# Own rows left unscaled between the second and third pass of a four-layer graph kernel, and the squares shared by two engines

## The reference, cut to what matters

```
scores = h_src @ a_s + h_tgt @ a_t
mx = segment_max(scores, tgt);  ex = exp(scores - mx[tgt]);  se = segment_sum(ex, tgt)
agg = segment_sum(h_src * (ex / (se[tgt] + 1e-10))[:, None], tgt)
h_combined = h + agg
h_poincare = tanh(|h_combined|) * h_combined / |h_combined|     # per row
result = h_poincare, or h_poincare * 0.95 / (|h_poincare| + 1e-8) where the norm is over 0.95
```

## Time and profile before

| | |
|---|---|
| device time, median of 3 | 4950.73 us (4947.53 to 4952.23) |
| profiled execution: span from first to last instruction | 5717.0 us |
| what lies around that span in the profiled execution | not listed; its own time is read as the span |
| busy shares PE, PE weight load, DVE, ACT, POOL | 58%, 38%, 57%, 32%, 58% |
| mean granted TensorE clock | 0.754 |
| POOL, line 527 (own rows scaled) | 49 instructions, 44.1 us busy |

### The profile page before, as it was taken

How to read it: one execution, slowest core, us unless ns; L and a number is a source line. 1 busy time by engine, 2 the same in 40 slices (tenths; PEclk the granted TensorE clock), 3 DMA queues, 4 the chain that set the end, 5 groups by cost and what they waited for, 6 DMA issues and landing times. The chain is left out here.

```text
span 5717.0 us, 56211 instructions
## 1 busy us (share of the span) xinstructions
PE 3330.2 (58%) x11120; PEld 2187.6 (38%) x11120; DVE 3248.6 (57%) x10255; ACT 1811.1 (32%) x4253; POOL 3290.0 (58%) x3410
## 2 busy tenths in 40 slices
PE   0477777777543555556554555555555556666555
PEld 0355555555431333333333333333333334333333
DVE  8677777777983555555566344444447344334435
ACT  2254444444692323333336322222226100000000
POOL 5566666666004666666653666666662466666664
PEclk8789988898875777776777767777777776667767
DMA  2444444443114333333333444444443433333333
GB/s 90 118 110 111 110 110 107 110 111 106 49 46 123 92 91 93 94 89 93 92 101 119 111 111 113 114 112 112 114 111 114 143 98 99 93 98 101 99 91 107
DMA packets 290665, 586.90 MB, mean 103 GB/s; under 512 B 63201, under 2 KB 170717, under 8 KB 290334
## 3 DMA queue, kind: packets, MB, share of 16 engines
q0 software_dynamic: 159456, 440.74, 29.6%
q1 hardware_dynamic: 100322, 108.64, 6.1%
q10 hardware_dynamic: 30556, 33.94, 2.1%
HBM read 530.98 MB, written 52.10 MB: 102 GB/s over the span
## 5 line engine op out<-in xcount | busy, mean ns | idle before, releaser
L519 POOL DMA_INDIRECT X<-table,src_tab x2490 | 2367.7, 951 | 1786.5 <-issue 690.4
L639 PE MATMUL psum<-X,onehot 128*128 128x259 f32 x4980 | 1906.8, 522 | 1245.7 <-DVE A L1280 570.9
L639 PEld LDWEIGHTS psum<-X,onehot 128*128 128x128 f32 x4980 | 1118.2, 251 | 1827.8 <-issue 1117.1
L1280 DVE SCALAR_TENSOR_TENSOR A<-A,psum 128x259 f32 x1660 | 701.7, 423 | 1315.4 <-remote 690.8
L1280 DVE SCALAR_TENSOR_TENSOR A<-A,same_tab,psum 128x259 f32 x1620 | 777.0, 480 | 613.4 <-remote 308.3
L509 POOL DMA_INDIRECT X<-table,src_tab x832 | 793.7, 954 | 534.0 <-issue 233.1
L780 ACT ACTIVATE onehot<-G,zero_col,ecols 128x128 f32<-128x128 bf16 x1660 | 697.3, 482 | 987.6 <-remote 325.5
L648 PE MATMUL psum<-H,G 128*128 x1664 | 602.9, 450 | 352.9 <-DVE G L1368 208.9
L626 PE MATMUL psum<-X,onehot 128*128 128x259 f32 x1664 | 559.3, 422 | 4.4 <-DVE A L1280 3.1
L648 PEld LDWEIGHTS psum<-H,G 128*128 128x128 f32 x1664 | 318.1, 215 | 545.5 <-issue 510.0
L780 ACT ACTIVATE onehot<-onehot,zero_col,coef 128x128 f32<-128x128 bf16 x832 | 350.6, 482 | 277.3 <-DVE coef L1411 83.7
(11 more groups left out here) (367 smaller groups left out, 2843.4 us busy)
## 6 DMA issues: line engine op xcount, KB each, us to landing
X<-table,src_tab POOLq DMA_INDIRECT x3322
plain<-rows_dram ACTq DMA_DIRECT2D x168, 160.0 KB
plain<-rows_dram SPq DMA_DIRECT2D x104, 256.0 KB
table<-H SPq DMA_DIRECT2D x21, 906.5 KB, 5.9
x_dram<-X SPq DMA_DIRECT2D x21, 896.0 KB, 4.1
X<-x_dram SPq DMA_DIRECT2D x14, 896.0 KB, 6.1
table<-A SPq DMA_DIRECT2D x7, 906.5 KB, 7.0
G<-x_dram SPq DMA_DIRECT2D x7, 896.0 KB
```

The lines of the kernel that those rows point to most:

```text
L519: pool.indirect_dma_start(ring[:, s % SLOTS, :], None, table, bass.IndirectOffsetOnAxis(src_tab[:, s:s + 1], 0)).then_inc(sem(f"batch_in{s ...
L639: pe.matmul(psum[:, k % ACC_BANKS, 0:W], hots[:, k % HOTS, :], ring[:, k, :], start=True, stop=True).then_inc(sem("used"), 1)
L1280: stt(total, total, same, psum[:, t % ACC_BANKS, 0:W], ALU.mult, ALU.add).then_inc(sem("sum_added"), 1)
```

## The change

The own rows are no longer multiplied. With own' = be (1 + share), A = A * kk + H * be is written as be * (A * (kk / be) + H): `merge_shares` makes kk / be and keeps be, combine uses the raw H, the sums of squares are multiplied by be squared, and the row factor t1 by be. POOL has no part in it. ScalarE takes the squares of blocks 0 to 35 (SQ_ACT = 36), VectorE those of 36 to 48, each right behind the next block's combine. The branches for several ranges in MERGES, empty before, are gone.

```diff
-MERGES = ((0, NB),)
+SQ_ACT = 36
@@ gpsimd
-            def scale_own(lo, hi):
-                pool.wait_ge(sem("shares"), len(MERGES))
-                for b in range(lo, hi):
-                    pool.tensor_scalar(H[:, b, 0:D], H[:, b, 0:D], col("be")[:, b:b + 1], None, ALU.mult).then_inc(sem("own_scaled_late"), 1)
                 gathers(q)
-                if q == 0:
-                    scale_own(*MERGES[-1])
@@ scalar
-            merge_parts(len(MERGES) - 1)
-            for m, (lo, hi) in enumerate(MERGES):
-                for b in range(lo if m == len(MERGES) - 1 else ..., hi):
-                    square_sum(b)
+            merge_exps()
+            for b in range(SQ_ACT):
+                square_sum(b)
@@ vector, merge_shares
                 chain(tt(t2, A[:, :, AUX], over, ALU.mult))
                 chain(tt(t2, t2, own, ALU.add))
                 chain(ts(t2, t2, 1e-10, None, ALU.add))
-                chain(dve.reciprocal(t2, t2))
-                chain(tt(over, over, t2, ALU.mult))
+                chain(tt(own, own, t2, ALU.add))
+                chain(dve.reciprocal(own, own))
+                chain(tt(over, over, own, ALU.mult))
+                dve.reciprocal(t2, t2)
+                chain(dve.reciprocal(own, own))
                 chain(tt(own, own, t2, ALU.mult))
-                ts(own, own, 1.0, None, ALU.add).then_inc(sem("shares"), 1)
@@ vector, combine
-                    dve.wait_ge(sem("own_scaled_late"), b - MERGES[-1][0] + 1)
                 stt(A[:, b, 0:D], A[:, b, 0:D], col("kk")[:, b:b + 1], H[:, b, 0:D], ALU.mult, ALU.add).then_inc(sem("combined"), 1)
+            def square_combined(b):
+                dve.wait_ge(sem("combined"), b + 1)
+                stt(junk[:, b % UN, :], A[:, b, 0:D], 1.0, A[:, b, 0:D], ALU.mult, ALU.mult,
+                    accum_out=col("aa")[:, b:b + 1]).then_inc(sem("squared_dve"), 1)
@@ vector, after the pass
-            merge_shares(len(MERGES) - 1)
-            for b in range(*MERGES[-1]):
+            merge_shares()
+            for b in range(NB):
                 combine(b)
+                if b > SQ_ACT:
+                    square_combined(b - 1)
+            square_combined(NB - 1)
...
-            dve.wait_ge(sem("squared"), 5 * NB)
+            tt(col("t4"), col("be"), col("be"), ALU.mult).then_inc(sem("share_square"), 1)
+            dve.wait_ge(sem("share_square"), 1)
+            dve.wait_ge(sem("squared_dve"), NB - SQ_ACT)
+            dve.wait_ge(sem("squared"), 4 * NB + SQ_ACT)
+            chain(tt(col("aa"), col("aa"), col("t4"), ALU.mult))
             scalar_func(ts(col("f0"), col("aa"), MIN_NORM ** 2, None, ALU.max))
...
             chain(tt(col("t1"), col("t1"), col("t4"), ALU.mult))
+            chain(tt(col("t1"), col("t1"), col("be"), ALU.mult))
```

More of the change, by code:

```diff
@@ L879, in elu_parts, with merge_exps @@
                     func(H[:, b - 1, 0:D], H[:, b - 1, 0:D], ACT.Exp, scale=-1.0).then_inc(sem("elu_exp"), 1)
[L881 to L902, removed]
+            def merge_exps():
+                act.wait_ge(sem("gaps"), 1)
+                func(col("kk"), col("kk"), ACT.Exp)
+                func(col("be"), col("be"), ACT.Exp).then_inc(sem("gap_exps"), 1)
             def weighted(q):
@@ L923, in turn @@
                             weigh(q, i, h * GR + k)
-                            if q == 0:
-                                merges(s)
                             if q == 1 and s >= LT + ELU_LAG:
@@ L1076, in _ @@
             weighted(0)
-            for m, (lo, hi) in enumerate(MERGES[:-1]):
-                for b in range(max(lo, lo + S_REAL - LT - hi - 8), hi):
-                    scale_own(m, b)
-            merge_parts(len(MERGES) - 1)
-            for m, (lo, hi) in enumerate(MERGES):
-                for b in range(lo if m == len(MERGES) - 1 else max(lo, lo + S_REAL - LT - hi - 14), hi):
-                    square_sum(b)
+            merge_exps()
+            for b in range(SQ_ACT):
+                square_sum(b)
             asked(20)
@@ L1716, in fade_first, with merge_gaps @@
                 chain(stt(blk(A, at, AUX3, W), blk(A, at, AUX, AUX + 1), drop, blk(A, at, AUX3, W), ALU.mult, ALU.add))
[L1718 to L1722, removed]
+            def merge_gaps():
+                z, peaks = A[:, :, AUX], A[:, :, AUX3]
+                t2, t3, over, own = (col(name) for name in ("t2", "t3", "kk", "be"))
                 ts(t3, z, 0.5, -BIG, ALU.is_lt, ALU.mult)
@@ L1727, in merge_gaps @@
                 chain(tt(t2, t2, t3, ALU.add))
-                chain(tt(t3, H[:, lo:hi, AUX2], H[:, lo:hi, AUX3], ALU.max))
+                chain(tt(t3, H[:, :, AUX2], H[:, :, AUX3], ALU.max))
                 chain(tt(t3, t3, t2, ALU.max))
                 tt(over, t2, t3, ALU.subtract)
[L1731 to L1738, removed]
+                tt(own, H[:, :, AUX2], t3, ALU.subtract).then_inc(sem("gaps"), 1)
@@ L1739, in merge_shares @@
+            def merge_shares():
+                dve.wait_ge(sem("gap_exps"), 1)
+                t2, over, own = (col(name) for name in ("t2", "kk", "be"))
+                chain(tt(t2, A[:, :, AUX], over, ALU.mult))
                 chain(tt(t2, t2, own, ALU.add))
                 chain(ts(t2, t2, 1e-10, None, ALU.add))
-                chain(dve.reciprocal(t2, t2))
-                chain(tt(over, over, t2, ALU.mult))
+                chain(tt(own, own, t2, ALU.add))
[3 more added lines that the diff above has]
+                chain(dve.reciprocal(own, own))
@@ L1743, in merge_shares @@
                 chain(tt(own, own, t2, ALU.mult))
-                ts(own, own, 1.0, None, ALU.add).then_inc(sem("shares"), 1)
             def combine(b):
-                if b < MERGES[-1][0]:
-                    dve.wait_ge(sem("own_scaled"), b + 1)
-                else:
-                    dve.wait_ge(sem("own_scaled_late"), b - MERGES[-1][0] + 1)
                 stt(A[:, b, 0:D], A[:, b, 0:D], col("kk")[:, b:b + 1], H[:, b, 0:D], ALU.mult, ALU.add).then_inc(sem("combined"), 1)
[L1753 to L1762, removed]
+            def square_combined(b):
+                dve.wait_ge(sem("combined"), b + 1)
+                stt(junk[:, b % UN, :], A[:, b, 0:D], 1.0, A[:, b, 0:D], ALU.mult, ALU.mult,
+                    accum_out=col("aa")[:, b:b + 1]).then_inc(sem("squared_dve"), 1)
@@ L1973, in _ @@
             softmax_sums()
[L1975 to L1978, removed]
-            merge_shares(len(MERGES) - 1)
-            for b in range(*MERGES[-1]):
+            merge_gaps()
+            merge_shares()
+            for b in range(NB):
                 combine(b)
+                if b > SQ_ACT:
+                    square_combined(b - 1)
+            square_combined(NB - 1)
             dve.wait_ge(sem("vectors_in"), 16 * 5)
```

## The result

The changed kernel took 4918.58 us (median of 4, 4914.18 to 4919.88) against 4950.69 us before: a ratio of 0.9935, 95% interval 0.9923 to 0.9947. That is 32.1 us less.

What follows compares the result with a forecast made beforehand. No engine bounds the whole; POOL's 49 scalings pace the stretch between second and third pass. Line 1988 coming 19.05 us earlier, less 0.25 us for a longer chain, gave 18.8 us less: 4950.73 to 4931.9 us, range 4923 to 4942.

Steps and rivals of the forecast that it cites:

- rival 2: Stretch between passes: DVE keeps 0.70 us a combine even without POOL's work; 4.1 us gained, 4946.6 us; chance 0.04.
- rival 1: Same stretch: ACT sets the end because its squares keep 0.90 us; 11.5 us gained, 4939.2 us; chance 0.06.
- rival 4: Third transform: TensorE's clock stays low, 49 blocks cost 54 us, less the 18.8; slower, 4986 us; chance 0.03.
- Rival 3: Third and fourth pass: give half or more of the gain back as gathers fall otherwise; 4941 to 4951 us; chance 0.06.
- What is late next: Step on what follows the stretch: x's read covered by 26 us, later work moves as a whole, POOL's queue off the path.
- The term that stood at nothing: Passes behind the stretch: third pass's gathers follow the transform and move as a whole; no gain counted there.

## Why the prediction was wrong

**What held.** The stretch was forecast to start its combines at 2.87 us behind the first column operation of the shares; it was 2590.76 - 2587.96 = 2.80. The combines run at 482 ns, 0.40 apart (nine in 3.65 us), not at 0.70: rival 2 falls, and POOL's work beside them was what had made them long: with 49 scratch scalings beside them, for which they do not wait, some take up to 721 ns again. Combines and squares on DVE were to take 24.15 us and took 2614.66 - 2590.76 = 23.90. ACT's squares start (2608.5 - 2591.3) / 35 = 0.49 us apart and end 5.7 us ahead of DVE, with the table load hidden: rival 1 falls. The root is asked for 29.06 us behind the shares' start (2617.02 - 2587.96) where it was 48.43 in the earlier trace rows: 19.4 us gained where 19.05 were forecast, before the 0.25 us of the longer chain. From first combine to first addition it is 31.5 us for 50.4 in the earlier trace rows. The third transform went as before (70 and 71 us, mean granted clock 0.91 and 0.90): rival 4 falls. Rival 3 had the right place, the later passes, with the wrong sign.

**The step that failed** is in "What is late next": "POOL's queue only loses: behind the scalings stands its wait for the transform's stores, so it is not on the path." It priced POOL's scalings by the time they took in the stretch, and the queue behind them by its start alone, and rival 3 was argued away with "nothing in them changes but their start". The duration of what is queued changed. The 1660 gathers behind the scalings took 7 to 8 ns more each than those ahead of them, and as POOL paces the passes nearly all of it counted: 49 scalings of unused data put back into the changed kernel brought 15.4 us, some 12 of them in the passes, and one product behind them in the kernel before took 10 to 12 us away. The term that stood at nothing, the later passes, measured 12 to 15 us (15.4 less the 3 in the stretch; 14.9 between the two profiled executions). 18.8 forecast plus 13.3 (1660 x 8 ns) are 32.1 us, which is what was measured; the sum is that exact by luck, as the 3 ns between executions show. What in POOL makes a gather longer stays open.

**What would have shown it** is a comparison of one line between stages: the same gather ahead of the scalings and behind. The prediction took the unusual length of its profiled execution as a reason to read differences only, but looked at no difference in the passes.

## What to carry to other kernels

Where one instruction repeats thousands of times and paces a pass, compare its duration from pass to pass in the profile, to the nanosecond: 8 ns were 13 us here. An operation that is taken off an engine can change the instructions that stay on it, so a removed operation is priced by its own time, by the contention beside it, and by what runs behind it. Before moving such work for that reason alone, try a single cheap operation of another kind behind it; here a product of two tensors helped, a fill and a copy did not.

## What the runs showed of the hardware

- On POOL an indirect gather of 128 rows takes 946 or 949 ns in most passes, and 953 to 960 behind runs of `tensor_scalar` (6 or 49 of them behind a pass at the normal level, in 7 executions without exception; 2 in one of two cases, 1 in none of two). It lasts as long as was seen, up to three passes with 2490 gathers, unless a `tensor_tensor` product comes: seen within an execution twice (960 to 949), and in the kernel before. A fill and a converting copy leave it (one run each). 49 products don't bring it (one run).
- It came once without scalings (957 ns in a first pass). What it is inside POOL is open; no run here shows it.
- DVE's multiply-add with two SBUF inputs takes 482 ns alone and 693 to 696 in the median beside POOL's scalings, which keep their 0.90 us from start to start. The Trainium skill, SBUF — State Buffer, Terms ("shared port pair"), has the loser blocked for the whole instruction; the trace does not agree, the multiply-add lost 0.21 us of POOL's 0.91.
